# The second half of a round taken sequence by sequence: the second sequence's low-rank stage and q, k, v issued inside the first one's attention

## The chip, the core and the metric

One core of one Trainium2 chip. The metric is the device time of one execution in microseconds; the median of several executions counts. Times inside the kernel are read from one profiled execution.

## What is computed

Eight sequences of 256 tokens with 256 channels go through four sublayers, each of the form x = x + LayerNorm(f(LayerNorm(x))):

```python
x = x + _layernorm(_L0_attn_ref(_layernorm(x)))   # state-space mixer (32 heads), then a gated FFN of width 1024
x = x + _layernorm(_L0_ffn_ref(_layernorm(x)))    # x @ W.T plus a low-rank part: 8 experts of rank 16, top 2 by softmax
x = x + _layernorm(_L1_attn_ref(_layernorm(x)))   # causal attention, 16 heads of 16 channels, q, k, v, o with biases
x = x + _layernorm(_L1_ffn_ref(_layernorm(x)))    # router over 64 experts, top 4, plus a shared gated FFN of width 512
```

## The kernel before

**Tiling.** The program takes the tokens in four rounds of 512, that is two sequences (halves j = 0 and 1 of 256 tokens, two tiles of 128 tokens each), and then runs one tail for all routed experts. A round has these stages: input projections and the mixer with its 32 heads; the gated FFN; the low-rank layer; q, k, v; attention; router and shared FFN. At the end of a round GpSimd scatters the normed rows with sixteen indirect DMAs (L1403); the same engine then masks the decay rows of the next round's mixer (L1391), in that order in its queue.

**What sets the order.** Each engine has one hand-written instruction list for a round, in the functions `tensor`, `scalar`, `gpsimd`, `vector`; a wait at the head of a list holds everything behind it. PSUM is handed out by `BankPlan`: `plan.use(key, bank)` gives a result its bank and its turn in it, `before` waits until the earlier user of the bank is drained, `full` until the result is there, `drained` until it has been read. Norms are made on VectorE: statistics (L1497, L1501), the variance to `ve` (L1486, `ask`), the power -1/2 on GpSimd (L1364), a wait for it (`answered`), and the scaling (L1512). The residual stream is `x1`.

**FFN (L953 to L970).** TensorE transposes u of both halves, then makes gate `G` and up `U` for each of eight blocks f over all 512 tokens, then `F` (down) for half 0 and half 1. ScalarE applies Silu (L1267), VectorE multiplies (L1632).

**Low-rank (L973 to L992).** For each half: transposes, one product `L` of 392 columns per tile (256 of W, 8 logits, 128 of the low-rank input). VectorE picks two of eight experts (L1650 to L1676), needing one Exp from ScalarE (L1276, L1284), scales the low-rank input into `hw` (L1678); TensorE turns it (`LT`) and adds it into `L` with `w_lb` (L991). VectorE then runs residual norm and next norm (L1686 to L1697).

**q, k, v (L995 to L1019).** Transposes of u ("att"), q and k per channel chunk for both halves, v per half.

**Attention (L1102 to L1123 on TensorE).** 32 steps n, one head of one sequence each; the first sixteen are sequence 0. TensorE takes two steps in each pass g: `scores`, the transposes of probabilities of two passes ago (`turn_probs`, L1047), and in every even pass from 4 on `add_o` (L1062, L1065). VectorE finds the negated row maximum of step n (L1789), ScalarE the exponentials (L1315), both copy turned probabilities (L1323, L1750). VectorE's loop also holds, at n = 2 to 14, the input norm of the next round (`ahead_...`, L1420 to L1448), and at n = 22 to 32 the output and norms of sequence 0. S has four banks, PT two.

**End of the round (L1127 to L1170).** `shared_hidden(0)` and `project_o(1)`, the transposes of the router's input of half 1, `route(1)`, `shared_hidden(1)`, `shared_down(0)`, the positions (`pos`), `shared_down(1)`, and the transposes for the next round (T "mix"). VectorE picks four of 64 experts from `route(1)` on (L1821 to L1863); its last result `sidx` starts the scatter.

## Time and profile before

| what | value |
|---|---|
| times of three runs | 1378.28, 1378.88, 1387.94 us; median 1378.88 |
| the profiled execution's own time | 1388.41 us |
| its span | 1386.6 us |
| mean granted TensorE clock | 0.883 of full speed |
| busy: TensorE, VectorE, ScalarE, GpSimd | 81%, 63%, 42%, 18% of the span |
| a round | 304 us, four of them; the tail takes the last 143 us |

The profiled execution is 1.8 us longer than its span and 9.5 us longer than the median of the three. Rounds two to four repeat one another to some hundredths of a microsecond in their long waits, so one is read: the third, 636 to 940 us. A timeline row gives start, duration, engine, line, operation, output and inputs, count, and in brackets the idle time of the engine before it and what ended it.

### The profile page before, as it was taken

The page shows a single profiled execution, that of the slowest core. Times are in us where ns is not written, and L with a number is a line of the kernel's source. Part 1 is how long each engine was busy: PE and PEld are TensorE (multiplying, and loading weights), DVE is VectorE, ACT ScalarE, POOL GpSimd, SP SyncE. Part 2 cuts the span into 40 slices and gives each one's busy share as a digit, 9 for nine tenths or more (in the row PEclk, how much of TensorE's full clock was granted, in tenths as well). Part 3 has the DMA queues.
Part 4 walks back from the last instruction along what each step waited for, and adds up shares of the span by engine and source line. Part 5 has one row for each costly group of instructions (what it writes and reads, how often), then busy time and mean ns, then how long its engine had stood idle before and what let it go on. Part 6 is the DMA issues. An engine that isn't in the chain of part 4 may idle for free.

```text
span 1386.6 us, 21861 instructions
## 1 busy us (share of the span) xinstructions
PE 1117.8 (81%) x6368; PEld 677.6 (49%) x6368; DVE 880.2 (63%) x2031; ACT 587.8 (42%) x1577; POOL 244.9 (18%) x429
## 2 busy tenths in 40 slices
PE   5999987979998978888998979889998979854500
PEld 2444555655444556574445546564445545542200
DVE  5999245756998155757996265668994357541187
ACT  3766213625665214616665116527664127423100
POOL 3222001005221011005221010015220000023211
PEclk9999997989999987989999978999999978976555
DMA  5898000003432000003331000003330060016664
GB/s 190 296 287 266 1 16 1 2 1 111 131 121 69 0 15 1 2 6 129 116 124 37 0 16 1 2 32 122 124 116 12 1 197 2 1 62 151 167 217 148
DMA packets 79707, 114.20 MB, mean 82 GB/s; under 512 B 10499, under 2 KB 69641, under 8 KB 78688
## 3 DMA queue, kind: packets, MB, share of 16 engines
q1 hardware_dynamic: 73296, 100.71, 23.2%
q10 hardware_dynamic: 2304, 8.39, 1.9%
q0 software_dynamic: 3984, 3.62, 0.9%
q8 instruction: 56, 0.92, 0.3%
q14 instruction: 67, 0.55, 0.1%
HBM read 92.39 MB, written 27.98 MB: 87 GB/s over the span
## 4 chain that ended last, share of the span: by engine, by line
issue 52%; PE 22%; DVE 10%; POOL 6%; DMA 4%; ACT 4%; SPq 2%; POOLq 0%; ACTq 0%; DVEq 0%
PE bank L803 10%; DVE hf L1549 3%; POOL rs L1364 3%; PE bank L1135 2%; DVE tmp L647 2%; DMA dec<-cum_dram 2%; PE bank L890 2%; PE bank L906 2%; PE bank L1148 2%; POOL xg_dram L1403 1%; ACT dec L1241 1%; DMA hn<-xg_dram 1%; ACT dec L1243 1%; PE bank L816 1%; POOL rs L1369 1%
## 5 line engine op out<-in xcount | busy, mean ns | idle before, releaser
L1549 DVE SCALAR_TENSOR_TENSOR hf<-bank,conv_w,hf 128x510 f32<-128x510 f32 (+2 forms) x384 | 278.1, 744 | 19.1 <-ACT hf L1197 13.8
L803 PE MATMUL bank<-uT,w_in 128*128 128x512 f32 x560 | 272.0, 614 | 14.0 <-DVE hf L1549 11.9
L1197 ACT ACTIVATE hf<-bank,conv_b,conv_w 128x512 f32<-128x512 f32 x128 | 99.4, 776 | 129.6 <-PE bank L803 129.6
L803 PEld LDWEIGHTS bank<-uT,w_in 128*128 128x128 f32 x560 | 97.0, 189 | 107.1 <-issue 76.5
L1364 POOL TENSOR_TENSOR rs<-ve,half 128x2 f32<-128x2 f32 x56 | 38.9, 695 | 556.5 <-DVE ve L1486 556.5
L1315 ACT ACTIVATE dec<-bank,nmax 128x128 f32<-128x128 f32 (+1 forms) x256 | 105.5, 425 | 62.0 <-DVE nmax L1789 62.0
L890 PE MATMUL bank<-hf 64*128 64x256 f32 x512 | 89.7, 427 | 10.6 <-ACT x_pad L1230 6.4
L803 PE MATMUL bank<-uT,w_gu 128*128 128x512 f32 x224 | 96.8, 592 | 0.0
L1789 DVE TENSOR_REDUCE nmax<-bank 128x1 f32<-128x128 f32 (+1 forms) x256 | 74.6, 350 | 31.1 <-PE bank L1039 30.1
L1632 DVE TENSOR_TENSOR hf<-xc,bank 128x512 f32<-128x512 f32 x32 | 22.0, 688 | 103.9 <-PE bank L803 77.1
L1183 ACT ACTIVATE uT<-bank 128x512 f32<-128x512 f32 x24 | 14.3, 596 | 165.1 <-PE bank L794 165.1
L1403 POOL DMA_INDIRECT xg_dram<-xf,sidx x64 | 63.1, 986 | 105.5 <-DVE sidx L1863 65.4
L1047 PE MATMUL bank<-ident,dec 128*128 128x128 f32 x384 | 66.6, 313 | 18.0 <-ACT turned_p L1323 9.6
L890 PEld LDWEIGHTS bank<-hf 64*128 64x128 f32 x512 | 38.6, 185 | 67.4 <-issue 60.0
L794 PE MATMUL bank<-ident,u 128*128 128x128 f32 x136 | 28.5, 353 | 51.7 <-DVE u L1512 23.6
L803 PEld LDWEIGHTS bank<-uT,w_gu 128*128 128x128 f32 x224 | 42.6, 190 | 51.8 <-issue 51.6
L1602 DVE TENSOR_TENSOR turned_p<-dec,bank 128x768 f32<-128x768 f32 x64 | 61.0, 953 | 10.6 <-ACT dec L1243 6.7
L1047 PEld LDWEIGHTS bank<-ident,dec 128*128 128x128 f32 x384 | 51.5, 162 | 29.4 <-issue 9.1
L1135 PE MATMUL bank<-uT,w_sgu 128*128 128x256 f32 x256 | 64.2, 411 | 0.0
L968 PE MATMUL bank<-w_dn,hf 128*128 128x256 f32 x256 | 56.2, 381 | 3.6 <-issue 3.6
L1135 PEld LDWEIGHTS bank<-uT,w_sgu 128*128 128x128 f32 x256 | 52.8, 209 | 9.2 <-issue 1.3
L1267 ACT ACTIVATE xc<-bank 128x512 f32<-128x512 f32 x32 | 19.1, 597 | 85.9 <-PE bank L803 76.0
(258 smaller groups left out, 2128.6 us busy)
## 6 DMA issues: line engine op xcount, KB each, us to landing
x<-cum_dram SPq DMA_DIRECT2D x32, 384.0 KB, 3.5
tmp<-cum_dram SPq DMA_DIRECT2D x32, 384.0 KB, 3.6
hf<-cum_dram SPq DMA_DIRECT2D x32, 384.0 KB, 3.6
dec<-cum_dram SPq DMA_DIRECT2D x32, 384.0 KB
y_dram<-xf SPq DMA_DIRECT2D x16, 512.0 KB, 6.0
hf<-y_dram ACTq DMA_DIRECT2D x16, 512.0 KB, 3.8
w_in<-in_w_egu SPq DMA_DIRECT2D x10, 512.0 KB, 9.0
w_in<-in_w_in SPq DMA_DIRECT2D x1, 3584.0 KB, 12.6
```

The lines of the kernel that those rows point to most:

```text
L803: mm = pe.matmul(plan[key][0:n, :], w[:, k, cols], uT[:, k, :], start=k == 0, stop=k == DC - 1)
L890: pe.matmul(both_cb[b][:, e, 0:SEQ], B[:, o:o + P], C[:, o:o + SEQ], start=True, stop=True)
L968: mm = pe.matmul(plan[("F", j)][:, i * D:(i + 1) * D], hf[:, f, t * P:(t + 1) * P], w_dn[:, f, :], start=f == 0, stop=f == FF // P - 1)
L1047: mm = pe.transpose(plan[key][:, i * P:(i + 1) * P], pr[:, n % 6, i * P:(i + 1) * P], ident[:, :])
L1135: mm = pe.matmul(plan[key][:, i * HALF:(i + 1) * HALF], w_sgu[:, k, o + i * P:o + (i + 1) * P], uT[:, k, j * HALF:(j + 1) * HALF], start=k ...
L1197: act.activation(dst, plan[key][:, :], ACT.Identity, bias=conv_b[:, j:j + 1], scale=conv_w[:, j, TAPS - 1:TAPS]).then_inc(tap0.sem, 1)
L1315: ins = act.activation(pr[:, n % 6, cols], plan[("S", n)][:, cols], ACT.Exp, bias=nmax[:, n % 4, i:i + 1], accum_out=esum[:, b, o:o + 1])
L1364: pool.tensor_tensor(rs[:, cols], ve[:, cols], half[:, cols], ALU.pow).then_inc(rstd_ready.sem, 1)
L1403: pool.indirect_dma_start(out=xg_dram, out_offset=bass.IndirectOffsetOnAxis(ap=sidx[:, i:i + 1], axis=0), in_=xf[:, i // TOPK, :], in_offs ...
L1549: ins = dve.scalar_tensor_tensor(d, x, conv_w[:, j, TAPS - 1 - s:TAPS - s], d, ALU.mult, ALU.add)
L1602: dve.tensor_tensor(sc[g % 4], dec[:, d:d + 2, :], both_cb[b][:, :, 0:TRI], ALU.mult).then_inc(plan.drains(("CB", p, b)), 1)
L1789: ins = dve.tensor_reduce(nmax[:, n % 4, i:i + 1], plan[("S", n)][:, cols], AX.X, ALU.max, negate=True)
```

## The change

No arithmetic is removed. The FFN, the low-rank layer and q, k, v are written per half (256 columns at a time), and their order is new:

- The FFN's `GU` (gate and up of 256 tokens side by side in one bank, banks 4, 5, 6 in turn) replaces `G` and `U`. Half 0 goes through all eight blocks, then half 1, with `F` of half 0 and the low-rank product of half 0 placed between blocks of half 1.
- `L` is split: `LA` (logits and low-rank input, 136 columns) and a new `L` that adds W and the low-rank part in one group. `hw`, `hwT` lie in `tmp`.
- q, k, v of half 0, then transposes and `LA` of half 1, stand ahead of the first scores. Everything else of half 1, up to v, is issued within passes 1 to 7 of attention, through the one bank 7. The input norm of the next round moves from n = 2 to 14 to n = 18 to 24 of VectorE's loop.
- Of a norm, the question to GpSimd and the wait for its answer are separate calls in more places; ScalarE now goes Silu, Exp, Silu within the FFN.
- At the end `shared_down(0)` stands ahead of the transposes and `route(1)`; VectorE's two `shared_gate(0, g)` stand inside the last norms.

```diff
-        for f in range(FF // P):
-            plan.use(("G", f), 4 + f % 2)
-            plan.use(("U", f), f % 2)
+        for j in range(2):
+            for f in range(FF // P):
+                plan.use(("GU", f, j), 4 + (8 * j + f) % 3)
...
+        for key in (("T", "lora", 1), ("LA", 1), ("LT", 1), ("L", 1), ("T", "att", 1), ("Q", 1), ("K", 1), ("V", 1)):
+            plan.use(key, 7)
...
-            plan.use(("S", n), n % 4)
-            plan.use(("PT", n), 4 + n % 2)
+            plan.use(("S", n), 3 + n % 4)
+            plan.use(("PT", n), 1 + n % 2)
...
# TensorE
+                for f in range(FF // P):
+                    gate_up(f, 0)
+                    if f == 3:
+                        transposes(pe, "ffn", 1, u, 1, r)
+                gate_up(0, 1)
+                ffn_down(0)
+                for f in (1, 2, 3):
+                    gate_up(f, 1)
+                pe.wait_ge(w_sem["lora"], 32)
+                transposes(pe, "lora", 2, u, 0, r)
+                gate_up(4, 1)
+                lora_in(0)
+                for f in (5, 6, 7):
+                    gate_up(f, 1)
+                lora_turn(0)
+                lora_out(0)
+                ffn_down(1)
+                pe.wait_ge(w_sem["att"], 32)
+                transposes(pe, "att", 3, u, 0, r)
+                project_att(0, "Q", 0)
+                project_att(1, "K", 0)
+                project_v(0)
+                transposes(pe, "lora", 2, u, 1, r)
+                lora_in(1)
+                clear_o(0)
...
+                    if g == 1:
+                        lora_turn(1)
+                    if g == 2:
+                        lora_out(1)
+                    if g == 4:
+                        transposes(pe, "att", 3, u, 1, r)
+                    if g == 5:
+                        project_att(0, "Q", 1)
+                    if g == 6:
+                        project_att(1, "K", 1)
+                    if g == 7:
+                        project_v(1)
...
+                shared_down(0)
                 transposes(pe, "moe", 4, xf, 1, r)
                 route(1)
                 shared_hidden(1, (0, 1))
-                shared_down(0)
...
# ScalarE, loop over n
+                    if n == 1:
+                        lora_weights(1)
+                    if n == 4:
+                        lora_turned(1)
+                    if n == 10:
+                        turned("att", 1, r)
+                    if n == 12:
+                        queries(1)
+                    if n == 14:
+                        keys(1)
...
# VectorE
+                for f in range(FF // P):
+                    gate(f, 0)
+                gate(0, 1)
+                n = ffn_moments(0)
+                gate(1, 1)
+                n = ffn_sum(0, n)
+                gate(2, 1)
+                next_norm(0, n)
...
+                n = lora_moments(0)
+                n = lora_sum(0, n)
+                next_norm(0, n)
+                link(take_shift(0, "att"))
+                n = ffn_moments(1)
+                n = ffn_sum(1, n)
+                next_norm(1, n)
+                link(take_shift(1, "lora"))
+                values(0)
...
+                    if n == 1:
+                        lora_choice(1)
                     if n == 2:
+                        lora_mix(1)
+                    if n == 3:
+                        lora_scaled(1)
+                    if n == 6:
+                        asked = lora_moments(1)
+                    if n == 7:
+                        asked = lora_sum(1, asked)
+                    if n == 8:
+                        next_norm(1, asked)
+                    if n == 9:
+                        link(take_shift(1, "att"))
+                    if n == 17:
+                        values(1)
+                    if n == 18:
                         ahead_stats(r + 1)
```

TensorE from the end of the FFN on, before. `w_gu` are gate and up weights, `w_dn` down, `w_lora` the low-rank layer's; `REGISTER_ALU` prepares a wait.

```order
L803 MATMUL bank4_5<-uT,w_gu 128x512 x2
L803 MATMUL bank1<-uT,w_gu 128x512 x2
L962 REGISTER_ALU
L968 MATMUL bank2_3<-w_dn,hf 128x256 x32
L791 REGISTER_ALU
L794 MATMUL bank4_5<-ident,u 128x128 x4
L976 REGISTER_ALU
L980 MATMUL bank0<-w_lora,uT 128x392 x2
```

The same place after:

```order
L976 MATMUL bank0<-w_dn,hf 128x256 x16
L965 MATMUL bank4_5<-uT,w_gu 128x256 x8
L962 REGISTER_ALU
L965 MATMUL bank6<-uT,w_gu 128x256 x4
L791 REGISTER_ALU
L795 MATMUL bank2_3<-ident,u 128x128 x4
L962 REGISTER_ALU
L965 MATMUL bank4_5<-uT,w_gu 128x256 x4
L983 REGISTER_ALU
L988 MATMUL bank2_3<-w_lora,uT 128x136 x4
```

Before, the whole `F` of half 1 stood between `F` of half 0 and the transposes of the normed half 0; after, three blocks `GU` of half 1 do.

VectorE at the first steps of attention, after. `nmax` is the row maximum of a step, the lines from L1744 to L1774 the choice and mixing of half 1's low-rank experts.

```order
L1935 TENSOR_REDUCE nmax<-bank4_5 128x1 x2
L1761 TENSOR_TENSOR wsum<-wk 128x2
L1567 REGISTER_ALU
L1762 RECIPROCAL wsum<-wsum 128x2
L1567 REGISTER_ALU
L1763 SCALAR_TENSOR_TENSOR wk<-wk,wsum 128x2x2
L1567 REGISTER_ALU
L1766 TENSOR_TENSOR oh0<-oh0,wk 128x32
L1567 REGISTER_ALU
L1769 TENSOR_TENSOR wm<-oh0 128x16
L1567 REGISTER_ALU
L1935 TENSOR_REDUCE nmax<-bank4_5 128x1 x2
```

Before, these small operations stood ahead of the first score's maximum, in the low-rank stage; after, the maxima of later steps queue behind them.

TensorE at the end of the round, before (`w_sgu` and `w_sdn` are the shared FFN's weights, `w_rt` the router's):

```order
L1135 MATMUL bank2_3<-uT,w_sgu 128x256 x4
L790 REGISTER_ALU
L794 MATMUL bank7<-ident,xf 128x128 x4
L1096 MATMUL bank7<-w_rt,uT 128x64 x4
L1132 REGISTER_ALU
L1135 MATMUL bank0<-uT,w_sgu 128x256 x4
```

and after:

```order
L1194 MATMUL bank6<-uT,w_sgu 128x256 x4
L1202 REGISTER_ALU x2
L1203 REGISTER_ALU
L1207 MATMUL bank1<-w_sdn,hf 128x256 x8
L791 REGISTER_ALU
L792 REGISTER_ALU
L795 MATMUL bank7<-ident,xf 128x128 x4
L1137 REGISTER_ALU
```

The down product of half 0 has moved from behind the shared FFN's hidden products of half 1 to ahead of the router's transposes.

## Rows read from the trace of the kernel before

**Rows 1.** Windows: length, busy PE, PEld, DVE, ACT, POOL (count), clock, DMA
```profile
751.50:841.80 90.30, 75.46 (x239) 48.38 (x239) 33.46 (x123) 19.00 (x40) 6.95 (x10) 0.85 0.02 6
841.80:898.40 56.60, 49.38 (x416) 31.73 (x415) 39.46 (x129) 34.76 (x146) 3.41 (x4) 0.88 0.01 1
898.40:930.40 32.00, 27.68 (x127) 23.72 (x127) 20.67 (x54) 5.46 (x8) 1.39 (x2) 0.89 0.05 18
```
**Rows 2.** Timeline of TensorE, FFN to the first scores
```profile
754.01 1.11 PE L794 MATMUL bank<-ident,u 128*128 128x128 f32 x4 [2.52 <-DVE u L1626]
...
787.06 14.05 PE L968 MATMUL bank<-w_dn,hf 128*128 128x256 f32 x64 [0.89 <-issue]
...
824.74 1.11 PE L794 MATMUL bank<-ident,u 128*128 128x128 f32 x4 [3.10 <-DVE u L1512]
...
841.80 0.49 PE L1033 MATMUL bank<-sz,xc 32*128 32x128 f32 x4
```
**Rows 3.** Timeline of VectorE: first and last step of two norm chains
```profile
794.24 0.69 DVE L1639 TENSOR_TENSOR h<-bank,h 128x512 f32<-128x512 f32 x1 [7.28 <-PE bank L968]
...
800.40 0.74 DVE L1512 TENSOR_SCALAR u<-x,mv,rs 128x256 f32<-128x256 f32 x2 [0.81 <-POOL rs L1364]
...
818.38 0.75 DVE L1497 BATCH_NORM_STATS2 stats<-bank 128x6 f32<-128x256 f32 x2
...
823.88 0.73 DVE L1512 TENSOR_SCALAR u<-x,mv,rs 128x256 f32<-128x256 f32 x2 [0.81 <-POOL rs L1364]
```
**Rows 4.** Windows of one microsecond (columns as in rows 1): two falls
```profile
753.00:754.00 1.00, 0.00 (x0) 0.00 (x0) 0.66 (x3) 0.17 (x2) 0.31 (x1) 0.91 0.03 8
...
760.00:761.00 1.00, 1.00 (x5) 0.81 (x4) 0.00 (x0) 0.00 (x0) 0.00 (x0) 0.68 0.00 0
...
844.00:845.00 1.00, 0.23 (x2) 0.00 (x0) 1.00 (x4) 1.00 (x6) 0.00 (x0) 1.00 0.00 0
...
846.00:847.00 1.00, 1.00 (x6) 0.30 (x4) 1.00 (x7) 0.78 (x4) 0.00 (x0) 0.50 0.00 0
...
856.00:857.00 1.00, 1.00 (x18) 0.68 (x12) 0.58 (x2) 0.64 (x4) 0.00 (x0) 0.89 0.00 0
```
**Rows 5.** Timeline of ScalarE: the table load for an Exp
```profile
809.74 1.28 ACT L1276 ACT_TABLE_LOAD   x1
811.03 0.21 ACT L1276 ACTIVATE wk<-wk 128x4 f32<-128x4 f32 x1
```
**Rows 6.** Groups of VectorE in attention, 841.8 to 898.4
```profile
L1789 DVE TENSOR_REDUCE nmax<-bank 128x1 f32<-128x128 f32 x64 | 18.7, 350 | 7.8 <-PE bank L1039 7.5
...
L1440 DVE TENSOR_SCALAR hn<-xin,mv,r 128x256 f32<-128x256 f32 x4 | 1.5, 406 | 0.0
L1420 DVE BATCH_NORM_STATS2 stats<-xin 128x6 f32<-128x256 f32 x4 | 1.4, 413 | 0.0
L1448 DVE TENSOR_SCALAR u<-hn,rs 128x256 f32<-128x256 f32 x4 | 1.2, 349 | 0.0
```
**Rows 7.** Timeline of TensorE: start of pass 8 and of pass 13
```profile
863.11 0.49 PE L1033 MATMUL bank<-sz,xc 32*128 32x128 f32 x4
...
879.26 0.49 PE L1033 MATMUL bank<-sz,xc 32*128 32x128 f32 x4
```
**Rows 8.** Timeline, end of the round: TensorE
```profile
910.84 1.12 PE L794 MATMUL bank<-ident,xf 128*128 128x128 f32 x4 [3.54 <-DVE xf L1512]
...
926.69 3.70 PE L1148 MATMUL bank<-w_sdn,hf 128*128 128x256 f32 x16
```
**Rows 9.** The same stretch: VectorE
```profile
914.70 0.29 DVE L1817 COPY lgt<-bank 128x128 f32<-128x128 f32 x1 [2.53 <-PE bank L1096]
...
924.17 1.28 DVE L1808 TENSOR_TENSOR hf<-xc,bank 128x512 f32<-128x512 f32 x2 [0.20 <-DVE lk L1844]
...
930.65 0.17 DVE L1863 CAST sidx<-slot 128x16 uint32<-128x16 f32 x1
```
**Rows 10.** Timeline of GpSimd: first mask of the next round, behind the last scatter
```profile
952.29 0.77 POOL L1391 TENSOR_SCALAR_AFFINE_SELECT x<-x 128x256 f32<-128x256 f32 x2
```

More of the change, by code:

```diff
@@ L1646, in _, with next_norm, lora_choice @@
                     keep_shift(j)
-                    norm(tiles(x1, H[j]), u, H[j]).then_inc(u_ready.sem, 1)
-                for j in range(2):
-                    dve.wait_ge(lora_lg.sem, lora_lg.at(r, 2 * j + 2))
+                    return moments(tiles(x1, H[j]), H[j])
+                def next_norm(j, n):
+                    answered(n)
+                    normed(tiles(x1, H[j]), u, H[j]).then_inc(u_ready.sem, 1)
+                def lora_choice(j):
+                    dve.wait_ge(lora_lg.sem, lora_lg.at(r, j + 1))
                     settle(dve)
@@ new lines, in lora_moments, with lora_sum @@
+                def lora_moments(j):
+                    dve.wait_ge(*plan.full(("L", j), r))
+                    return moments([plan[("L", j)][:, i * D:(i + 1) * D] for i in range(2)], H[j])
+                def lora_sum(j, n):
+                    answered(n)
+                    for i in range(2):
+                        t = 2 * j + i
+                        ins = dve.scalar_tensor_tensor(x1[:, t, :], plan[("L", j)][:, i * D:(i + 1) * D], rs[:, t:t + 1],
+                                                       x1[:, t, :], ALU.mult, ALU.add)
+                    ins.then_inc(plan.drains(("L", j)), 1)
+                    dve.wait_ge(*plan.drained(("L", j), r))
```

394 lines of the change are left out of this document (207 added, 187 removed).

## The prediction, made before the changed kernel ran

> **What bounds the kernel now.** I read the page for the shares of the engines, then windows by stage, then timelines of one round, then the groups of attention. The windows split a round's second half into 90.3 us from the mixer's end to the first scores, 56.6 us of attention and 32 us of the end [rows 1]. In the first of them TensorE is named busy for 75.5 us at a clock of 0.85, VectorE for 33.5, ScalarE for 19. No engine is full; TensorE carries the chain and stops where a norm must come back: before transposes it waits 2.52, then 3.10 us [rows 2]. What such a wait costs is more than its length. After 0.77 us of idleness in one microsecond, and some more in the next, the granted clock was 0.50 from 846 and full again only within 856; another fall went from 753.8, behind the wait of 2.52 us, into 760 [rows 4]. At 0.50 (1.2 GHz) each matmul takes twice its time at 1.00 (2.4 GHz). So the stage is a chain of TensorE work, norms and half-speed stretches.
>
> In attention three engines turn in one ring. VectorE has 18.7 us of row maxima there, plus 1.4 for the statistics, 1.5 and 1.2 for the scalings of the look-ahead norm [rows 6], and is busy 39.5 of 56.6 us; TensorE is named busy 49.4 us [rows 1]. The question is how much room attention has for half 1's chain.
>
> **Step 1, to the first scores: a gain.** I rebuild TensorE's list with its own durations. A 256-column f32 matmul takes 14.05 / 64 = 0.22 us at full clock [rows 2], and four transposes take 1.11 us at half clock, so 0.56. Up to the first scores stand 128 matmuls for gate and up (28.2 us), 64 for down (14.05), 12 for `L` of half 0 (2.6), 24 for q, k, v of half 0 (5.3), five sets of transposes (2.8) and, an estimate by columns, two `LA`, one `LT` and the zeroing (3.4). Sum 56.4 us.
>
> Then its waits. The start up to the first gate is unchanged in kind (0.9 us for ScalarE's copy). The norm chain of half 0 goes from the add at 794.24 to the end of u at 801.14, 6.9 us [rows 3]. Before, `F` of half 1 (7 us) covered it. After, three blocks `GU` (24 matmuls, 5.3 us) cover it, so with 0.4 us of handing over the wait is 2.1 us. Before `LT` TensorE waits some 0.9 us for choice, Exp and scaling. The chain of `L` (818.38 to 824.61, 6.2 us [rows 3]) lies under `F` of half 1 (7 us). Half 1's own norm chain (6.9 us) begins when `F` ends, and under it lie transposes, a copy and q, k, v (0.6 + 0.8 + 5.3): 0.5 us of wait is left, with two copies of 0.8. Waits together: 6 us.
>
> Then the clock. The half-speed stretch from the start of the FFN stays (2.8 us lost). The new wait of 2.1 us is longer than the one around 845 that the clock answered, so I take one more fall, and 3.4 us lost by it (half of the 6.8 us from 753.8 to 760.6 [rows 4]). Sum 56.4 + 6 + 6.2 = 68.6 us from 754.0, so first scores at about 822 against 841.8 [rows 2]: 19.8 us gained a round, and 23.2 if the new fall doesn't come.
>
> The two table loads added in ScalarE's list (Silu, Exp, Silu) cost 1.28 us each, and the Exp started 0.01 us behind such a load [rows 5]; they lie beside blocks f = 5 to 7 and are in the 0.9 us above. The Trainium skill ("ScalarE: Activation LUTs", What ACT_TABLE_LOAD costs) adds a drain of 1.38 us to each switch, 2.66 us in all. The trace does not agree: nothing stands between load and Exp here. By the page `LT` would be 2.8 us later in each round, 11 us in all, and the total 1395 us.
>
> **Step 2, passes 0 to 8 of attention: a loss.** From the first score to pass 8 it was 21.3 us [rows 2, 7]. I follow the new lists from the first score as 0. VectorE: maximum 0 at 1.2 to 1.8, choice (1.25), maximum 1, mixing (1.0), maximum 2, scaling, done at 5.7. TensorE has scored four steps by 2.3 and stands at `LT` until 5.8: 3.5 us idle, and the clock falls. At half clock it does pass 2 and most of `L` of half 1 (12 matmuls), full at about 13.6. VectorE has had nothing to do for 3.6 us, since its moments of `L` stand ahead of maximum 6. Its chain then runs with the ring behind it: ask at 15, sum and next ask at 18.5, maximum 7 and the copy of probabilities 3 at 19.5, u at 20.2. TensorE in pass 4 needs that copy: idle 2.6 us, a second fall. Pass 5 ends at 26. From here TensorE is the bound, with q, k, v of 1.75 us each and passes of 1.1 + 0.8 us (and `add_o` 0.8 in every second): pass 8 starts at 36.0, without the second fall at 34.1. Loss 14.7 or 12.8 us.
>
> The new work alone is 8.8 us of TensorE (36 matmuls and six transposes) and about 8.8 us of VectorE (2.7 for choice, mixing and scaling, 6.2 - 1.6 for the chain [rows 3], 1.5 for shift and values), against 5.3 us that the look-ahead norm frees. A bound from below for the loss is then 3.5 us (everything fits between), from above 8.8 + 8.8 = 17.6 (nothing does). I take 13.7, near the upper end, because one-bank hand-overs put TensorE, ScalarE and VectorE behind one another.
>
> **Step 3, passes 8 to 13.** It was 16.15 us [rows 7]. VectorE had some 10 us of work there (ten maxima of 18.7 / 32 us [rows 6], five copies, reciprocals, one output); the look-ahead norm (5.3 with its small operations) and `values(1)` (0.9) make it 16. The statistics at n = 18 and the reciprocals at n = 19 delay the copy that pass 10 needs: 2.6 us of idleness on TensorE, a fall, and the delayed spreading of inverses. I get 20.3 us with the fall, 18.7 without: a loss of 4.2 or 2.6; I take 3.4. From pass 13 on nothing changes in attention.
>
> **Step 4, end of the round: a loss.** Before, TensorE idled 3.54 us before the router's transposes [rows 8], the result reached VectorE at 914.70, and from there VectorE's chain ran without cover to the gates (925.4) and `sidx` (930.8) [rows 9]. TensorE had the hidden products and `shared_down(0)` to fill that time, and `shared_down(1)` began at 926.69, 1.3 us after the gates. Now `shared_down(0)`, 3.5 us, needs both gates of half 0, which VectorE gives at 909.9 between the norms. It fills 0.9 us of the idle time and pushes transposes, router and everything behind by 2.7 us at full clock; by some 2 us more if the clock falls in the 2.7 us of idleness before it, as it did before (1.12 us for four transposes [rows 8]). I take +3 us for `sidx`. Behind the positions TensorE has nothing left, waits some 3 us for the gates, and begins `shared_down(1)` at half clock: +4.7 us for the next round's transposes. The two paths into the next mixer were level: the first mask at 952.29 came directly behind the last scatter [rows 10], which follows `sidx`, and ScalarE, which follows the transposes, was ready within a microsecond of it. So the later one counts. I take 4 us a round, between 2.5 and 6.
>
> **Sum.** -19.8 + 13.7 + 3.4 + 4 = +1.3 us a round, four rounds +5 us, on 1388.4 us of the profiled execution 1393.6; on the median of 1378.9 it is 1384. Mixer and tail are taken as unchanged.
>
> **The rivals.**
>
> *The attention has room (faster).* The clock doesn't fall in step 1, the later falls in attention stay out, and the end costs its least: -23.2 + 12.8 + 2.6 + 2.5 = -5.3 us a round, -21 in all, 1358. For it: VectorE is idle 17 of 56.6 us in attention [rows 1], the freed first steps are where the new work goes, and 23 us per round is surely freed ahead of it. Against: TensorE's waits in the new lists are each longer than the one after which the clock fell at 846 [rows 4].
>
> *Half 1's chain becomes the bound of attention (slower).* Place: VectorE's list between n = 1 and n = 9, where maxima queue behind choice, moments and sums; price 14.7 + 4.2 us with both falls, and the end at its dearest, 6 us: -19.8 + 18.9 + 6 = +5.1 us a round, +20, 1399. It decides once attention takes over 17 us longer to its end than before. For it: 3.5 us of idleness so early puts the most expensive TensorE work of the stage (12 + 24 matmuls) into half-speed stretches. Against: each step of my schedule assumes the latest of three engines, and errors of that kind point one way.
>
> *The table switch drains* (the skill's rule above): 1395.
>
> **How the numbers follow.** A change under 1% (13.8 us) is about what a measurement of this kernel cannot tell from none. The forecast, within 1%, gets 0.43; attention with room 0.29; the chain as bound 0.25; the drain 0.03. That gives faster 0.29, same 0.43, slower 0.28. The range is from 1358 (the faster rival's value) to 1402 (the slower one's and three more for errors in mixer and tail).
>
> **What would show it.** Right: first scores some 68 us after the FFN's transposes instead of 88; a wait of about 2 us before the transposes of normed half 0; pass 0 to pass 8 about 35 us instead of 21.3, with 3 us of idleness before `LT` of half 1 and half clock after; pass 8 to 13 near 19.5 us; `shared_down(0)` directly behind the second gate of half 0, and first mask of the next round 4 us later from the end of attention; a round of about 305 us. Wrong: attention (first score to the spreading of inverses) under 68 us, TensorE's clock above 0.9 in it, or rounds under 300 us would speak for the first rival; rounds above 308 us for the second. If first scores come earlier than 64 or later than 74 us after the transposes, step 1 was mis-sized.

## The result: 1.6 per cent slower, and where a round went

The changed kernel took 1407.2 us (median; 1400.9 to 1410.2) beside 1379.9 for the kernel before. The ratio on record is 1.0156, 95% interval 1.0117 to 1.0194; the two medians divided give 1.0198. The forecast was 1384, within 1 per cent, so the kernel is slower than that. Of the range, 1358 to 1402, the outcome is at the upper edge: the ratio on the 1378.9 us that the forecast was made for gives 1400.4, just inside, and the median itself lies outside. Ratios here and below are over the executions on record as fast, so without one of E6 at 2308 us, which its median holds. The profiled execution took 1404.3 us, with a span of 1402.5, against 1388.4 of before.

First the windows of the third round by stage: first the changed kernel, then the kernel before, cut at the same events. The columns are length, busy PE, PEld, DVE, ACT and POOL with their counts, then TensorE's granted clock.

```profile
764.10:830.30 66.20, 59.88 (x269) 50.69 (x269) 25.97 (x91) 17.02 (x36) 4.35 (x7) 0.92 0.03 9
830.30:865.50 35.20, 29.34 (x191) 20.17 (x190) 18.77 (x71) 21.11 (x81) 1.38 (x2) 0.85 0.01 1
865.50:888.80 23.30, 20.80 (x143) 12.91 (x142) 15.49 (x54) 11.43 (x47) 2.14 (x2) 0.71 0.00 1
888.80:907.80 19.00, 14.59 (x122) 9.51 (x121) 12.20 (x38) 7.98 (x30) 1.39 (x2) 0.82 0.00 1
```

```profile
754.00:841.80 87.80, 75.46 (x239) 48.38 (x239) 31.94 (x119) 17.34 (x32) 6.23 (x9) 0.85 0.02 7
841.80:863.10 21.30, 19.93 (x149) 12.88 (x148) 16.38 (x60) 13.76 (x61) 2.02 (x2) 0.76 0.00 1
863.10:879.30 16.20, 14.75 (x144) 9.45 (x143) 10.89 (x32) 13.09 (x55) 0.00 (x0) 1.00 0.01 2
879.30:897.30 18.00, 13.60 (x122) 8.72 (x121) 12.19 (x38) 7.91 (x30) 1.39 (x2) 0.91 0.01 1
```

The four windows are: the FFN's first transposes to the first score, passes 0 to 8, passes 8 to 13, and pass 13 to the spreading of the second inverses (`EB` of sequence 1, "EB1" below). The first gives 21.6 us back; the other three take 14.0, 7.1 and 1.0. The loss in the third is the one to look at: TensorE is busy 6 us longer with the same 143 to 144 instructions, at a clock of 0.71 instead of 1.00.

**First scores.** The rows of TensorE that answer to [rows 2]:

```profile
764.06 0.66 PE L795 MATMUL bank<-ident,u 128*128 128x128 f32 x4 [2.52 <-DVE u L1709]
...
799.11 1.12 PE L795 MATMUL bank<-ident,u 128*128 128x128 f32 x4 [2.14 <-DVE u L1592]
...
830.26 0.49 PE L1079 MATMUL bank<-sz,xc 32*128 32x128 f32 x4
```

The wait before the transposes of normed half 0 is 2.14 us, as forecast, and the clock falls behind it. ScalarE's switches of table, which answer to [rows 5]:

```profile
806.21 1.28 ACT L1335 ACT_TABLE_LOAD   x1
807.50 0.21 ACT L1335 ACTIVATE wk<-wk 128x4 f32<-128x4 f32 x1
807.73 1.28 ACT L1326 ACT_TABLE_LOAD   x1
809.02 0.66 ACT L1326 ACTIVATE xc<-bank 128x256 f32<-128x256 f32 x2
```

Each costs 1.28 us, with the next instruction 0.01 us behind. The drain of 1.38 us that the Trainium skill ("ScalarE: Activation LUTs", What ACT_TABLE_LOAD costs) adds is not there in either direction.

**Passes 0 to 8.** TensorE, which answers to [rows 7]:

```profile
836.18 0.41 PE L996 MATMUL bank<-ident,tmp 128*128 128x128 f32 x2 [3.49 <-DVE tmp L1774]
...
850.06 0.77 PE L1093 MATMUL bank<-ident,dec 128*128 128x128 f32 x3 [1.89 <-DVE turned_p L1880]
...
865.55 0.49 PE L1079 MATMUL bank<-sz,xc 32*128 32x128 f32 x4
...
872.48 0.55 PE L1093 MATMUL bank<-ident,dec 128*128 128x128 f32 x3 [1.12 <-ACT hf L1411]
874.02 0.85 PE L1093 MATMUL bank<-ident,dec 128*128 128x128 f32 x3 [0.99 <-DVE hf L1880]
...
888.81 0.49 PE L1079 MATMUL bank<-sz,xc 32*128 32x128 f32 x4
```

The first row is the turn of half 1's scaled weights: 3.49 us idle, as drawn in step 2 (3.5). The second is the copy of probabilities that pass 4 waits for (1.89; forecast 2.6). Then come passes 8 to 13, with two short waits one behind the other, and behind them the clock (windows of one microsecond, columns as above, which answer to [rows 4]):

```profile
842.00:843.00 1.00, 1.00 (x4) 0.82 (x3) 0.00 (x0) 0.00 (x0) 0.00 (x0) 0.50 0.00 0
...
873.00:874.00 1.00, 0.03 (x1) 0.00 (x0) 0.97 (x4) 0.23 (x2) 0.00 (x0) 1.00 0.00 0
874.00:875.00 1.00, 0.98 (x7) 0.65 (x11) 0.90 (x6) 0.00 (x0) 0.28 (x1) 0.57 0.00 0
886.00:887.00 1.00, 1.00 (x6) 0.84 (x3) 0.00 (x0) 0.00 (x0) 0.00 (x0) 0.50 0.00 0
...
914.00:915.00 1.00, 1.00 (x4) 0.82 (x3) 0.00 (x0) 0.00 (x0) 0.00 (x0) 0.50 0.00 0
```

It stands at 0.50 from 874 into 887, 13 us in which TensorE has hardly a gap, and again at 914, in the end's hidden products. What VectorE did before the two waits (its timeline):

```profile
869.05 1.40 DVE L1508 BATCH_NORM_STATS2 stats<-xin 128x6 f32<-128x256 f32 x4
...
872.06 0.94 DVE L1875 RECIPROCAL h<-bank 32x128 f32<-32x128 f32 x1
...
873.43 0.54 DVE L1880 COPY hf<-bank 128x384 f32<-128x384 f32 x1
```

The look-ahead norm's statistics hold up the next maximum and with it ScalarE's Exp and copy (the 1.12 us wait); the reciprocal holds up the copy at 873.43, for which TensorE waits 0.99 us.

**End of the round.** TensorE and GpSimd, which answer to [rows 8] and [rows 10]:

```profile
907.83 1.68 PE L1121 MATMUL bank<-h,head_sel 32*128 32x256 f32 x4
909.45 6.49 PE L1194 MATMUL bank<-uT,w_sgu 128*128 128x256 f32 x16
...
923.90 5.40 PE L1207 MATMUL bank<-w_sdn,hf 128*128 128x256 f32 x16 [2.78 <-DVE hf L1864]
...
942.49 2.93 PE L1207 MATMUL bank<-w_sdn,hf 128*128 128x256 f32 x6 [3.39 <-DVE hf L1864]
```

```profile
968.33 0.79 POOL L1479 TENSOR_SCALAR_AFFINE_SELECT x<-x 128x256 f32<-128x256 f32 x2
```

From EB1 to the next round's first mask it is 60.5 us. Before it was 952.29 [rows 10] less 897.33, 55.0. Of the 5.5 us, 3.3 lie in the first hidden products and `project_o(1)`: the attended sum begins 9.9 us behind EB1 instead of 6.5, because 16 matmuls took 6.49 us at half clock. VectorE's rows, which answer to [rows 9], give the rest:

```profile
931.68 0.29 DVE L1953 COPY lgt<-bank 128x128 f32<-128x128 f32 x1 [6.87 <-PE bank L1142]
...
941.15 1.28 DVE L1864 TENSOR_TENSOR hf<-xc,bank 128x512 f32<-128x512 f32 x2 [0.20 <-DVE lk L1980]
...
946.64 0.17 DVE L1999 CAST sidx<-slot 128x16 uint32<-128x16 f32 x1
```

### The profile page after: what moved, and what is told of

Same layout as the page of the kernel before. It is cut to its first block, busy times and chain, and to the rows that moved or that the text cites. A ratio compares the mean times of both kernels' runs of the same rounds, so it can differ in the third digit from the quotient of the medians.

```text
span 1402.5 us, 22859 instructions
## 1 busy us (share of the span) xinstructions
PE 1129.0 (80%) x6656; PEld 736.7 (53%) x6656; DVE 884.9 (63%) x2063; ACT 609.1 (43%) x1633; POOL 245.6 (18%) x429
## 3 DMA queue, kind: packets, MB, share of 16 engines
q1 hardware_dynamic: 73296, 100.71, 23.1%
## 4 chain that ended last, share of the span: by engine, by line
issue 53%; PE 19%; DVE 12%; POOL 6%; DMA 4%; ACT 4%; SPq 1%; POOLq 0%; ACTq 0%; DVEq 0%
PE bank L804 10%; DVE hf L1629 3%; POOL rs L1452 3%; DVE tmp L648 2%; POOL xg_dram L1491 2%; PE bank L1207 2%; PE bank L891 2%; PE bank L907 2%; ACT dec L1300 2%; DMA dec<-cum_dram 1%; DMA hn<-xg_dram 1%; ACT dec L1302 1%; POOL rs L1457 1%; PE bank L817 1%; PE bank L892 1%
## 5 line engine op out<-in xcount | busy, mean ns | idle before, releaser
L965 PE MATMUL bank<-uT,w_gu 128*128 128x256 f32 x512 | 126.3, 408 | 3.7 <-ACT uT L1246 3.7
L965 PEld LDWEIGHTS bank<-uT,w_gu 128*128 128x128 f32 x512 | 104.9, 208 | 20.6 <-ACT uT L1246 4.8
L1093 PE MATMUL bank<-ident,dec 128*128 128x128 f32 x384 | 72.5, 331 | 31.3 <-ACT turned_p L1411 10.3
L1491 POOL DMA_INDIRECT xg_dram<-xf,sidx x64 | 63.3, 989 | 114.1 <-DVE sidx L1999 71.8
L1716 DVE TENSOR_TENSOR hf<-xc,bank 128x256 f32<-128x256 f32 x64 | 26.9, 420 | 86.4 <-ACT xc L1326 85.9
L1093 PEld LDWEIGHTS bank<-ident,dec 128*128 128x128 f32 x384 | 54.7, 170 | 43.3 <-DVE turned_p L1880 11.9
L1326 ACT ACTIVATE xc<-bank 128x256 f32<-128x256 f32 x64 | 24.1, 383 | 110.8 <-PE bank L965 110.8
L1194 PE MATMUL bank<-uT,w_sgu 128*128 128x256 f32 x256 | 68.8, 433 | 0.0
L1207 PE MATMUL bank<-w_sdn,hf 128*128 128x256 f32 x128 | 42.9, 509 | 24.7 <-DVE hf L1864 24.7
L1194 PEld LDWEIGHTS bank<-uT,w_sgu 128*128 128x128 f32 x256 | 55.9, 221 | 11.9 <-issue 2.6
L795 PE MATMUL bank<-ident,u 128*128 128x128 f32 x136 | 24.4, 315 | 37.3 <-DVE u L1536 16.5
```

What stands on the lines that cost most here:

```text
L965: mm = pe.matmul(plan[key][:, i * HALF:(i + 1) * HALF], w_gu[:, k, o:o + P], uT[:, k, j * HALF:(j + 1) * HALF], start=k == 0, stop=k == DC ...
L1093: mm = pe.transpose(plan[key][:, i * P:(i + 1) * P], pr[:, n % 6, i * P:(i + 1) * P], ident[:, :])
L1194: mm = pe.matmul(plan[key][:, i * HALF:(i + 1) * HALF], w_sgu[:, k, o + i * P:o + (i + 1) * P], uT[:, k, j * HALF:(j + 1) * HALF], start=k ...
L1207: mm = pe.matmul(plan[("SD", j)][:, i * D:(i + 1) * D], hf[:, f, t * P:(t + 1) * P], w_sdn[:, f, :], start=f == 0, stop=f == SHF // P - 1)
L1491: pool.indirect_dma_start(out=xg_dram, out_offset=bass.IndirectOffsetOnAxis(ap=sidx[:, i:i + 1], axis=0), in_=xf[:, i // TOPK, :], in_offs ...
```

## The experiments

In every table row the second round is cut at the same events; ratios are to the kernel before on the same chip, as recorded; quotients of medians differ from them by up to 0.7 per cent (0.977 for E2, 0.989 for E6). The chips differ: before took 1384.4 us beside E1 to E4, 1399.2 beside E5 to E8, 1401.6 beside E9 to E11 and 1386.2 beside E12. In the profiled executions of the two slower chips the mixer (last column) is 7 to 10 us a round longer than in comparable runs on the others, so totals are compared by their ratio. "T" are the FFN's first transposes, "S0" the first score. The kernel before was traced only on the chip of the result.

| run | T to S0 | passes 0-8 | 8-13 | 13-EB1 | EB1 to first mask | mask to next T | times before (95%) |
|---|---|---|---|---|---|---|---|
| before | 87.7 | 21.3 | 16.2 | 18.1 | 54.9 | 105.5 | 1 |
| changed | 66.2 | 35.3 | 23.3 | 19.0 | 60.5 | 106.4 | 1.0156 (1.0117-1.0194) |
| E1 old end | 64.4 | 33.3 | 23.1 | 19.0 | 58.6 | 105.5 | 1.0041 (1.0010-1.0072) |
| E2 early look-ahead | 63.3 | 33.2 | 16.6 | 17.9 | 55.6 | 107.0 | 0.9814 (0.9731-0.9897) |
| E3 half 1 first | 87.1 | 21.2 | 22.0 | 17.8 | 55.1 | 107.4 | 1.0226 (1.0181-1.0271) |
| E4 clock filled | 64.3 | 31.0 | 19.2 | 19.1 | 57.4 | 107.1 | 0.9823 (0.9778-0.9868) |
| E5 before, late look-ahead | 83.9 | 21.3 | 21.9 | 17.9 | 55.6 | 113.2 | 1.0156 (1.0088-1.0223) |
| E6 E2 + old end | 63.3 | 37.2 | 20.4 | 18.1 | 55.1 | 113.0 | 0.9823 (0.9745-0.9901) |
| E7 E6 + half 1 a pass later | 63.3 | 33.8 | 23.9 | 18.1 | 55.0 | 113.1 | 0.9854 (0.9782-0.9926) |
| E8 E6 + 17 fills | 61.6 | 31.0 | 16.6 | 19.0 | 55.1 | 115.3 | 0.9661 (0.9600-0.9723) |
| E9 changed again | 64.4 | 33.3 | 23.1 | 19.0 | 60.5 | 115.1 | 1.0124 (1.0076-1.0172) |
| E10 E8, new end | 63.2 | 31.0 | 16.6 | 17.9 | 57.3 | 115.3 | 0.9884 (0.9836-0.9931) |
| E11 E8 again | 63.2 | 31.0 | 16.6 | 18.1 | 55.1 | 112.9 | 0.9675 (0.9634-0.9716) |
| E12 half 1 first, look-ahead at 2-14 | 87.0 | 21.2 | 16.4 | 18.1 | 57.0 | 107.3 | 1.0100 (1.0066-1.0134) |

### E1: the old end of a round

```diff
                 shared_hidden(0, (1,))
-                shared_down(0)
                 transposes(pe, "moe", 4, xf, 1, r)
                 route(1)
                 shared_hidden(1, (0, 1))
+                shared_down(0)
```

(ScalarE's `shared_sum(0)` moves behind `shared_silu(1)` in the same way.)

> The changed kernel with the old end of a round: shared_down(0) behind shared_hidden(1), on ScalarE shared_sum(0) behind shared_silu(1). Theory: the new place of shared_down(0) sits on the path to the last index (its 5.4 us and the 2.78 us wait in front of it, partly at half clock, stand ahead of route(1)); undone, each round ends 2.2 to 3.6 us earlier, so 9 to 14 us less than the changed kernel's 1407: 1393 to 1398. R1 then reaches VectorE some 6 us earlier than now relative to project_o(1). Rival: what the end lost is only the half clock carried in from attention's last passes (3.3 us a round), which stays: 1403 to 1409.

Measured: 1389.5 us, 1.0041 times before. The end gives 1.85 us up to the mask and 0.89 behind it, 2.7 a round, inside the forecast of 2.2 to 3.6; the total is below the forecast's 1393 to 1398. The 3.3 us of half clock at its head stay (attended sum 9.9 us behind EB1), as the rival said of that part. The remaining gain, nearly 4 us in the second round, comes where nothing was changed: 1.8 us before the first scores and 2.0 in passes 0 to 8. There only the clock differs.

### E2: the look-ahead norm early

```diff
-                    if n == 18:
+                    if n == 10:
                         ahead_stats(r + 1)
-                    if n == 19:
+                    if n == 12:
                         ahead_moments(r + 1)
-                    if n == 20:
+                    if n == 14:
                         ahead_second_variance(r + 1)
...
```

(`ahead_layernorm` at 15 and 16, `ahead_rmsnorm` at 19 and 21.)

> The changed kernel with the look-ahead norm spread over n = 10 to 16 of VectorE's loop (its two u writes at 19 and 21), where VectorE waits 9 us for scores, instead of 18 to 24. Theory: the look-ahead norm in passes 9 to 12 is what makes TensorE wait (1.12 and 0.99 us) and brings the half clock from 874 to 888; moved, pass 8 to pass 13 takes 18 to 20 us instead of 23.3 and passes 0 to 8 stay at 35.3: 3 to 5 us a round, 1387 to 1395. Rival: passes 0 to 8 take over what the later ones lose (35.3 becomes 38 or more), or the waits at 872 and 874 come from the reciprocal and the index of the pass and stay: 1403 to 1409.

Measured: 1352.8 us, 0.9814. The theory held and was far too small (1387 to 1395 us, 18 to 20 us for passes 8 to 13): they fell by 6.7 us, to 16.6. Two windows of its second round, passes 0 to 8 and 8 to 13, and TensorE's wait for the copy behind the reciprocal:

```profile
504.48:537.65 33.17, 27.00 (x191) 18.62 (x191) 22.35 (x88) 21.24 (x81) 3.40 (x4) 0.90 0.01 2
537.65:554.24 16.59, 14.70 (x144) 9.52 (x143) 11.81 (x38) 11.24 (x47) 0.00 (x0) 1.00 0.00 1
```

```profile
545.00 0.55 PE L1093 MATMUL bank<-ident,dec 128*128 128x128 f32 x3 [1.00 <-DVE hf L1880]
```

The wait of 0.99 us from the changed kernel is still there (1.00). The 1.12 us one ahead of it is not, and the clock stays at 1.00. VectorE did 3.6 us more in passes 0 to 8 (22.35 against 18.77) and these became no longer. So the room that the first rival spoke of was there, in passes 5 to 8, where TensorE's products of half 1 keep VectorE waiting (in the changed kernel it is busy 4.45 of the 10.5 us from 855.0 to 865.5); the change put the look-ahead norm behind that room.

### E3 and E12: half 1's chain ahead of the first scores

```diff
                 lora_in(1)
                 clear_o(0)
+                lora_turn(1)
+                lora_out(1)
+                transposes(pe, "att", 3, u, 1, r)
+                project_att(0, "Q", 1)
+                project_att(1, "K", 1)
+                project_v(1)
```

(The same lines leave the loop of passes; ScalarE's and VectorE's lists follow, and LT, Q, K, V of half 1 use banks 6, 4, 5, 6.)

> The changed kernel with half 1's chain (choice, turn, L, norm, transposes, q, k, v) issued whole ahead of the first scores on every engine; banks 4 to 6 for its LT, Q, K and V; the look-ahead norm stays at 18 to 24. Theory (issuing inside attention hides part of the chain): first scores 19 to 23 us later than in the changed kernel (85 to 89 behind the FFN's transposes), passes 0 to 8 back at 21 to 23, passes 8 to 13 at 19 to 21 since values(1) is gone from them: 3 to 6 us a round more than the changed kernel, 1418 to 1430. Rival (inside attention each step of the chain waits its turn in the loop, and the falls of the clock eat what it hides): the same or less than the changed kernel, 1395 to 1408.

Measured: 1415.3 us, 1.0226, just below the theory's 1418 and not in the rival's range. First scores 87.1 us behind the transposes: the 21 us of step 1 are all postponement, and the new order of the FFN by itself is worth 0.6 us. Passes 0 to 8 are back at 21.2. Passes 8 to 13 stay at 22.0 with `values(1)` gone from them, where I had expected 19 to 21. So `values(1)` costs them little, and the look-ahead norm costs nearly everything:

```profile
856.30:877.50 21.20, 19.93 (x149) 12.86 (x148) 12.30 (x40) 14.00 (x62) 0.00 (x0) 0.76 0.00 1
877.50:899.50 22.00, 19.36 (x143) 12.09 (x142) 15.75 (x53) 13.25 (x55) 2.14 (x2) 0.77 0.01 2
```

VectorE is busy 15.75 of 22 us in the later passes and 12.30 in the earlier ones. E12 puts the look-ahead norm back to n = 2 to 14 as well:

> Half 1's chain whole ahead of the first scores, as in the third experiment, and the look-ahead norm at n = 2 to 14 as in the kernel before; the new order of the FFN and the new end of a round stay. Compared with the changed kernel with the look-ahead norm early (0.981 times the kernel before), it leaves only the placing of half 1. By the stages of the runs so far: first scores 87.0 behind the FFN's transposes, passes 0 to 8 21.3, 8 to 13 16.2, to EB1 17.9, the new end 2 to 4 us longer than the old one: 1.003 to 1.013 times the kernel before, so that placing half 1 inside attention is worth 2.2 to 3.2 per cent. Rival (the look-ahead norm among the first passes lengthens them when it stands there, or the new order of the FFN gives more than the 0.7 us a round seen): above 1.018, or below 0.998.

Measured: 1.0100, in the range. Passes 8 to 13 are 16.4 and passes 0 to 8 stay at 21.2 although they hold the norm (25.6 in the first round, where the clock is 0.60 instead of 0.76). Against E2 two things differ, the placing of half 1 and the steps at which the look-ahead norm stands (2 to 14, in E2 10 to 21); each has it where its stages don't grow by it. A round up to EB1 takes 142.7 us instead of 131.0: placing half 1 inside attention, with the norm placed to suit, is worth 11.7 us in this round and 2.9 per cent by the ratios, which come from two chips. The idea of the change was right.

### E4: the clock

```diff
+                FILL = {1: (12, 0), 3: (2, 0), 4: (2, 5), 9: (2, 2), 10: (2, 2), 12: (2, 2), 13: (2, 2), 14: (2, 2), 15: (2, 2), 16: (4, 4), 17: (4, 4)}
+
+                def fill(k, b):
+                    for _ in range(k):
+                        pe.matmul(plan[("OT", b)][:, :], zeros_bf[:, 0:P], zeros_bf[:, :], start=False,
+                                  stop=False, skip_group_check=True)
...
                     if g == 1:
+                        fill(FILL[1][0], 0)
                         lora_turn(1)
```

(And 2 to 8 a pass, ahead of its turns of probabilities, in passes 3, 4, 9, 10 and 12 to 17; `OT` of sequence 0 up to pass 10, of sequence 1 from 12. 61 a round.)

> The changed kernel with short products of zeros added to the output bank in front of TensorE's waits in attention (12 in front of the turn of half 1, 2 to 5 in front of the turns of passes 3, 4, 9, 10 and 12 to 17), about 0.22 us each at full clock; nothing else changes. Theory (the clock): the granted clock stays at 1.0 through 836 to 843, 850 to 854, 874 to 888 and 898 to 904, where it is 0.50 now; passes 8 to 13 take 17 to 19 us instead of 23.3, passes 0 to 8 take 31 to 33; 6 to 10 us a round less, 1367 to 1383. Rival (the chain of handovers on VectorE and ScalarE binds, the clock only takes up idle time): clock up, but 1403 to 1412.

Measured: 1361.7 us, 0.9823, better than the theory's best. Passes 0 to 8 and 8 to 13 of its second round:

```profile
513.26:544.27 31.01, 29.16 (x212) 19.23 (x211) 18.68 (x71) 21.20 (x81) 1.38 (x2) 1.00 0.01 2
544.27:563.50 19.23, 17.13 (x155) 10.81 (x154) 15.39 (x54) 11.38 (x47) 2.14 (x2) 1.00 0.01 2
```

The clock is 1.00 in both, with VectorE and ScalarE doing what they did in the changed kernel (18.68 and 15.39 us busy against 18.77 and 15.49 on VectorE). So of the 35.3 us of passes 0 to 8, at least 4.3 were the half clock; of the 23.3 us of passes 8 to 13, at least 4.1 were, and some 3 us above 16.2 are the hand-overs themselves. The fills don't hold the clock everywhere: in the first round passes 8 to 13 took 22.5 us at 0.85. The fill in the third round, and the wait behind it:

```profile
812.59 2.75 PE L1152 MATMUL bank<-zeros_bf 128*128 128x512 bf16 x12
816.25 0.41 PE L996 MATMUL bank<-ident,tmp 128*128 128x128 f32 x2 [0.90 <-DVE tmp L1784]
```

Twelve products of zeros take 2.75 us of the 3.49 us that TensorE would have waited, and cost nothing.

### E5: the kernel before with the late look-ahead norm alone

```diff
-                    if n == 2:
+                    if n == 18:
                         ahead_stats(r + 1)
...
```

(The whole block of the changed kernel, n = 18 to 24, in the kernel before.)

> The kernel before with one thing of the change alone: its look-ahead norm stands at n = 18 to 24 of VectorE's loop instead of 2 to 14. If the look-ahead norm is what lengthens passes 8 to 13 (22.0 us with half 1 first, 23.3 in the changed kernel, 16.6 with it early), passes 8 to 13 take 20.5 to 22.5 here instead of 16.15 and passes 0 to 8 stay at 21.3 or fall by at most 0.5; 4.5 to 6 us a round, 1400 to 1410. Rival (it hurts only beside values(1) or after a fallen clock): passes 8 to 13 below 18.5, 1384 to 1393.

Measured: 1421.5 us beside 1399.2, 1.0156: the one edit alone makes the kernel before as slow as the changed one, inside the forecast taken as a ratio (1400 to 1410 was written for 1384 us). Passes 0 to 8 at 21.3 and 8 to 13 at 21.9:

```profile
544.40:565.70 21.30, 19.93 (x151) 12.91 (x150) 11.94 (x39) 13.75 (x62) 0.00 (x0) 0.76 0.00 1
565.70:587.60 21.90, 19.05 (x144) 11.99 (x143) 15.69 (x53) 13.25 (x55) 2.18 (x2) 0.77 0.00 1
```

5.7 us a round, and nothing came back where the norm was taken away. It needs neither `values(1)` nor half 1 beside it. Ahead of the first scores this trace is 3.8 us shorter than that of the kernel before in three of four rounds, which nothing in the edit explains.

The mixer is where this chip is slower, and ScalarE's rows show the time. At the mixer's start it stands idle for up to 9 us at a stretch, and the profile names no engine that it waits for:

```profile
339.87 0.28 ACT L1212 ACTIVATE cum_tok<-bank 128x128 f32<-128x128 f32 x1 [2.68 <-remote]
349.68 1.27 ACT L1218 ACTIVATE sz<-bank,chan 128x512 f32<-128x512 f32 x2 [8.24 <-remote]
```

Such stops, named "remote" or "issue", stand in every mixer behind the first in E5 to E11. In the traces of the kernel before, the changed one, E1 to E4 and E12 none there is over 1 us. What ScalarE waits for is not shown.

### E6, E7 and E8: what else was left

> The changed kernel with the look-ahead norm at n = 10 to 16 and the old end of a round, the two undoings of the first two experiments together. If they add up (first scores 63.3, passes 0 to 8 33.2, 8 to 13 16.6, to EB1 17.9, from EB1 to the first mask 53.5, from there to the next round's transposes 105.5), a round takes 290 and the kernel 1333 to 1342. Rival: a clock fall that the early look-ahead norm had avoided lands elsewhere and takes up to 3 us a round back: 1343 to 1352.

Measured: 0.9823, beside 0.9814 for E2: the two repairs don't add up, and it is worse than even the rival allowed (1343 to 1352 us, 0.970 to 0.977 of the 1384 it was written for). The mixer's 6 us go with ScalarE's stops, as above. Up to EB1 the instructions are those of E2, and the waits too: 3.50 us before the turn of half 1 (3.51 in E2), 1.88 (1.89) in pass 4. Yet passes 0 to 8 took 37.2 us, not 33.2. E2's window behind its wait of 1.89 us, which ended at 523.14, then E6's behind its one of 1.88 us, which ended at 537.56:

```profile
524.00:525.00 1.00, 1.00 (x21) 0.56 (x9) 0.88 (x4) 0.70 (x3) 0.00 (x0) 1.00 0.00 0
```

```profile
537.00:538.00 1.00, 0.44 (x2) 0.44 (x3) 1.00 (x4) 0.84 (x4) 0.27 (x1) 0.50 0.00 0
...
545.00:546.00 1.00, 1.00 (x4) 0.82 (x3) 0.40 (x5) 0.72 (x4) 0.48 (x1) 0.50 0.00 0
```

The same wait left the clock alone in one and halved it for some 10 us in the other. In E6 passes 8 to 13 were hit too (20.4), behind the 1.01 us wait for the reciprocal's copy, which did nothing in E2. Neither the chip nor the edit has to be the reason, for the four rounds of one execution differ in the same way, with the same waits (1.9 us in pass 4; 1.0 us in pass 10, in E1 and E9 1.1 and 1.0):

| run | passes 0 to 8, rounds 1 to 4 | passes 8 to 13, rounds 1 to 4 |
|---|---|---|
| E1 | 33.3, 33.3, 33.3, 37.2 | 23.1, 23.1, 23.1, 23.0 |
| E2 | 33.2, 33.2, 33.1, 33.2 | 16.6, 16.6, 16.6, 16.6 |
| E6 | 37.2, 37.2, 37.2, 32.6 | 20.4, 20.4, 16.6, 20.4 |
| E9 | 37.2, 33.3, 33.2, 35.6 | 23.0, 23.1, 23.1, 23.3 |

> As the kernel with the early look-ahead norm and the old end, and each of half 1's PE steps behind the first scores one pass later (turn at pass 2, L at 3, transposes at 5, Q, K, V at 6, 7, 8), ScalarE and VectorE to match; look-ahead norm at 12 to 16, values(1) at 18. Theory: the 3.49 us wait before half 1's turn, and the half clock behind it, are there because one pass does not cover choice, table load and mix; with a pass between, the wait is under 1 us and passes 0 to 8 take 29 to 31.5 instead of 33.2: 1322 to 1334. Rival: K1 becomes ready only at pass 8's own turn, the wait moves there (2 us or more before scores 16): 1336 to 1348.

```diff
-                    if g == 1:
+                    if g == 2:
                         lora_turn(1)
-                    if g == 2:
+                    if g == 3:
                         lora_out(1)
...
```

Measured: 0.9854, no gain over E6, and 1383.7 us is outside both forecasts. The 3.49 us wait went and was replaced by two, which TensorE's timeline shows:

```profile
523.29 0.80 PE L1079 MATMUL bank<-yg,xc 32*128 32x128 f32 x4 [2.40 <-ACT dec L1403]
...
552.26 0.49 PE L1079 MATMUL bank<-sz,xc 32*128 32x128 f32 x4 [2.41 <-ACT yg L1355]
```

The first is the scores of pass 2, whose banks the Exps of steps 0 and 1 have to free, and the row maximum for the second of these stands behind VectorE's choice for half 1; the second is pass 8 itself, which waits for K of half 1, as the rival said.

> As the kernel with the early look-ahead norm and the old end, with 12 short products of zeros in front of half 1's turn and 5 in front of the second turn of pass 4, nothing else. Theory: the half clock behind the 3.49 us wait costs 2.2 us a round (31.0 for passes 0 to 8 against 33.2): 1324 to 1334. Rival: without these falls the later waits bring the clock down just as much, and nothing is left: within 3 us of the kernel without the products.

Measured: 0.9661, E6 with 12 fills before the turn of half 1 and 5 in pass 4. Passes 0 to 8 took 31.0 us in every round, and the gain over E6 on the same chip is 1.6 per cent, larger than the 2.2 us a round expected, since E6 had lost more there than E2. The total, 1355.4 us, is above the forecast's 1324 to 1334, as E6's was.

### E9, E10 and E11: the end once more, and the chip

> The changed kernel unaltered, beside the two that follow, since the kernel before took 1384 us on the chip of the first four experiments and 1399 on that of the next four. Expected of every theory: 1.012 to 1.020 times the kernel before. Rival (the ratio too is one of a chip): below 1.008 or above 1.024.

> The changed kernel with the early look-ahead norm and the 12 + 5 short products, with the new end of a round kept. Against the kernel that is the same but for the old end. If shared_down(0) ahead of route(1) costs 2 to 3.5 us a round whatever the clock does, this is 8 to 14 us slower than that one. Rival (the cost seen in the first experiment came with where the clock fell): within 4 us of it.

> The kernel of the early look-ahead norm, the old end and the 12 + 5 short products again, on this chip: 0.955 to 0.975 times the kernel before. If it is above 0.98, its gain was one of the chip or of where the clock happened to fall.

Measured on one chip: 1.0124, 0.9884 and 0.9675. E10 and E11 are alike up to EB1, the fills included, and differ in the place of `shared_down(0)` alone. TensorE's last products and the transposes for the next mixer, E10 and then E11, 31.3 and 29.5 us behind EB1:

```profile
609.68 6.41 PE L1217 MATMUL bank<-w_sdn,hf 128*128 128x256 f32 x16 [3.39 <-DVE hf L1874]
```

```profile
615.93 1.04 PE L795 MATMUL bank<-ident,u 128*128 128x128 f32 x8
```

```profile
604.18 3.70 PE L1217 MATMUL bank<-w_sdn,hf 128*128 128x256 f32 x16
607.71 1.04 PE L795 MATMUL bank<-ident,u 128*128 128x128 f32 x8
```

In E10 `shared_down(1)` stands idle for 3.39 us and then runs at half clock; in E11 `shared_down(0)` fills that wait. The transposes come 37.6 and 33.0 us behind EB1. The first mask is 2.2 us later and the mixer ends another 2.4 us later: 4.6 us in this round, and 2.1 per cent of the kernel between the medians, 28.9 us where 8 to 14 were expected. The two traces differ by 15.1 us in their spans: E10's profiled execution was its fastest, so half of the 28.9 us lies in executions without a trace. The first experiment's 2.7 us a round was the smaller figure.

E10 is also E2 with the 12 + 5 fills. It took 0.9884 of the kernel before and E2 0.9814 (0.9731 to 0.9897), on another chip, so there the fills show no gain: passes 0 to 8 are 2.2 us shorter in the second round, and the end is 1.7 us longer up to the mask.

## Why the prediction was right or wrong

**Step 1, right in kind, 1.8 us short.** Forecast: 68.6 us to the first scores, measured 66.2. (The sum carries on 19.8 us as the gain; 87.8 - 68.6 is 19.2, so 0.6 us a round are a slip. The real gain was 21.6.) The wait of 2.1 us came (2.14). The fall behind it was taken at 3.4 us lost; the windows of the changed kernel show the clock at 0.50 only from 799 into 802, half as much. In other rounds and runs of the same order the stretch took 61.6 to 66.2 us: in E4, with nothing altered in it, 66.2, 64.3, 63.3 and 63.3.

**Step 2, right.** Forecast +13.7, measured +14.0, with both waits where they were drawn (3.5 and 2.6 forecast, 3.49 and 1.89 measured). E4 divides it: with the clock at 1.00 it is +9.7 (31.0 us), between the bounds of 3.5 and 17.6, and the half clock is the other 4.3. The kernel before had a fall of its own there, 846 to 856 (a clock of 0.76), so at full clock on both sides the new work costs more than 9.7; with half of those 10 us, an estimate, up to 15. And the match to 0.3 us is partly luck: with the same waits the stage took 33.2 us in the first round of the changed kernel and 37.2 in the fourth of E1, so the clock alone moves the loss from 12 to 16.

**Step 3 failed.** "I get 20.3 us with the fall, 18.7 without: ... I take 3.4." It measured +7.1 (23.3 us). The cause was named rightly (statistics and reciprocal ahead of the copy that pass 10 needs). The size was not: I priced the fall as one of the usual length, 1.6 us lost, and it lasted from 874 into 887. E4 shows 4.1 us of the stage to be clock; E5 shows that the moved norm alone costs 5.7 us a round, 1.6 per cent, as much as the whole change. The deeper mistake stands in step 2: "against 5.3 us that the look-ahead norm frees". It freed nothing in passes 0 to 8. The kernel before holds the norm in those passes and E5 doesn't, and both take 21.3 us in all four rounds, though VectorE's busy time falls from 16.38 to 11.94 us; E12 and E3 repeat it at 21.2 (but for E12's first round).

**"From pass 13 on nothing changes in attention" failed by the clock.** +1.0 us there and +3.3 at the head of the end, both at half clock with unchanged instructions (16 hidden products in 6.49 us). In the second rounds of E2 and E4 the 3.3 us are not there: the attended sum stands 6.5 us behind EB1.

**Step 4, right in mechanism and size.** Forecast +4 (2.5 to 6), with an idle of 2.7 us before `shared_down(0)` (measured 2.78) and some 3 us before `shared_down(1)` (3.39). In the changed kernel the end grew by 5.5 to the mask, 3.3 of it not its own, and by 0.9 behind it: 3.1 us of its own. E10 against E11 gives 4.6 in the second round.

**Sum.** Forecast +1.3 us a round; measured in the second round -21.54 + 13.99 + 7.10 + 0.95 + 5.51 + 0.89 = +6.9. The gap of 5.6 us is the size of step 3 (3.7) and the clock from pass 13 to the attended sum (4.3), less what step 1 gave more (1.8) and step 4 cost less. The rounds are not alike, though. The first is 2.6 us longer than before, the second and third 6.9 and 6.7, and the last is 2.8 us shorter up to EB1, since its falls spared it 3 us ahead of the first scores; with the start and the end of the program that makes the 15.9 us between the two profiled executions. Up to EB1 the change is worth -3.6 to +0.5 us a round in this trace, and -4.9 in one round of E9, with the same instructions and waits; what it loses for certain is the end.

**The rivals.** "Attention has room" was given 1358 and was wrong for this change, yet E2 shows the room: 1353 us with the look-ahead norm in it. "Half 1's chain becomes the bound" was to decide once attention takes over 17 us longer to its end; it took 22.0 us longer, and a round over 308 us (310.6) was its mark. By these marks it is the rival that came true, and its 1399 is nearest to the 1400.4 of the result. But its place was wrong: step 2 stayed at its forecast, and the excess came behind pass 8. The drain of the table switch is excluded by the rows.

What stays open: what ScalarE waits for in the mixer on two of the chips, and which rounds the clock will hit. That E6 loses up to EB1 what E2 gains by clock alone is shown; when a wait brings a fall is not.

## What to carry to other kernels

A filler that was moved to make room has to be placed as carefully as what took its room: look for the stretch in which its engine waits for the others (here VectorE in passes 5 to 8), and move it alone to see its price. Work of another engine's chain that is issued inside a loop is worth it even when it makes the loop longer, but each wait it leaves costs its length and often half speed behind it, so compare the granted clock of a stage before its waits. Short products of zeros added to a bank that is being accumulated are a cheap test of that. As a remedy they helped here beside the old end (0.966 to 0.968 of the kernel before, with the early look-ahead norm) and showed no gain beside the new one (E10 against E2).
